# Row maxima of two heads in the two halves of TensorE's rows, later value products, and an unrolled expert loop

## The chip, the cores and the metric

The kernel runs on one core of a Trainium2 chip. The time is device microseconds of one execution of the whole program. TensorE (PE) multiplies, its weight loads are listed as PEld; VectorE is DVE, ScalarE is ACT, GpSimd is POOL, SyncE is SP and issues most DMAs. TensorE's clock has two levels, 1.2 and 2.4 GHz; a granted clock of 1.00 is the upper one.

## The reference, cut to what matters

A two-layer block over 4 sequences of 1024 tokens, width 256. Layer 0 is a linear attention and a mixture of 8 experts (2 for each token), layer 1 a causal softmax attention with 16 heads of 16 columns and a mixture of 16 experts (4 for each token) with a shared expert. The two parts that the change touches are

```python
# layer 1 attention: B=4, S=1024, 16 heads, d_head=16
scores = jnp.einsum('bqhd,bkhd->bhqk', Q, K)
scores = jnp.where(causal[None, None], scores, -jnp.inf)
attn = jax.nn.softmax(scores.astype(jnp.float32), axis=-1)
out = jnp.einsum('bhqk,bkhd->bqhd', attn, V).reshape(B, S, D)
# both layers, for each expert: 352 = 2*176 columns up, 176 down
h = silu(x @ w1[:, :176]) * (x @ w1[:, 176:])
y = h @ w2
```

The experts are computed on sorted tokens only: each tile of 128 tokens belongs to one expert, there are 71 such tiles in layer 0 and 143 in layer 1.

## The kernel before, in words

**Routed tiles** (`sparse_experts`, called for both layers). For each tile PE transposes x (2 instructions, L708), multiplies up (6 matmuls with 352 columns, L719), transposes h (2, L730) and multiplies down (6 with 256 columns, L742). Each fp32 product is three passes of high and low halves, which ACT and DVE split. The stages are staggered by `in_steps`: in step n PE does `transpose(n)`, `up(n-1)`, `transpose_h(n-2)`, `down(n-3)`. The matmuls read their weights at a register that holds the tile's expert. PE gets those registers from `te` with one TENSOR_LOAD (L694) at the head of each block of eight tiles: 8 registers at first, 11 in each turn of the hardware loop (`Fori`), 10 in the last part.

**Causal attention** (`causal_attention`). 16 rounds of 4 heads each (4 groups of heads, 4 sequences). In a round there are twelve steps of one 128-row key tile against one 512-column chunk of queries; of each step PE computes the four heads' scores (`scores`, L1508, up to 512 columns, three PSUM banks `psS`), ACT takes exp to `PT`, POOL cuts the diagonal (`cuts`), and PE multiplies by the values (`values`, L1520, four heads in four column groups of the array, 128 rows by 32 columns each). exp needs the maximum of each row, which is found a round ahead: *units* of at most one PSUM bank with queries as rows (`unit`, L1486 matmuls over 126 rows, of which 64 carry data, and a bf16 mask matmul L1493 for the diagonal), each reduced by DVE (L1399). There are 38 units for a round, 608 in all. The order within a step is written out by hand:

```python
ORDER = "0u1u2u3uv"     # digit: scores of that head, u: a unit of a later round, v: the values of the step before
```

Three slots hold the rounds' QS, KS and VA; `psM` has three banks, `psX` takes the transposes of the maxima (L1501) and of the outputs (L1535). After a round's last step the values of step 11, their copy to `OT` by DVE (L1424), the transposes and `divide` (L1429, L1433) follow before the next round begins. In step 6 DVE finishes the maxima of the next round (`whole`, L1408 and L1409) and PE transposes them. SP issues the loads (`pull`), the maxima's way through DRAM (`maxima_rows`) and the stores (`output`).

Of the kernel before, what the change touches and what calls it, by code (L numbers as in the profile page):

```python
# [12 lines left out]
F32 = mybir.dt.float32  # L13
# [169 lines left out]
def in_steps(eng, *stages, tiles=TILES, first=None, begin=None):  # L183
# [11 lines left out]
    if begin:  # L195
        begin(0, first)
    for n in range(first):
        step(n)
    with eng.Fori(first // POS_TILES, whole) as b:
        if begin:  # L200
            begin(b * POS_TILES, POS_TILES)
# [4 lines left out]
    if begin:  # L206
        begin(whole * POS_TILES, tiles + most - whole * POS_TILES)
# [438 lines left out]
def sparse_experts(nc, tag, E, NT, te, w_hi, w_lo, xs_dram, ys_dram, ident, shared=None):  # L646
# [3 lines left out]
    with phase(nc, shared) as (ctx, block):  # L650
# [37 lines left out]
        def _(pe):  # L688
            owners = {}

            def load_owners(n, count):
                before = 0 if isinstance(n, int) and n == 0 else 3
                count = min(count + before, NT - n + before) if isinstance(n, int) else count + before
                _, values = nc.values_load_multi_w_load_instructions(te[0:1, bass.ds(n - before, count)], (pe.engine,), min_val=0, max_val=E - 1,  # L694
                                                                      skip_runtime_bounds_check_because="a count of ends, cut to E - 1 where it is written")
                owners.clear()
                owners.update({j - before: v for j, v in enumerate(values)})

            def owner(i, lag):

                return owners[(i + lag) % POS_TILES - lag]
# [9 lines left out]
            def up(t, i, b):  # L711
                e = owner(i, 1)
# [20 lines left out]
            def down(t, i, b):  # L733
                e = owner(i, 3)
# [12 lines left out]
            in_steps(pe, (0, transpose), (1, up), (2, transpose_h), (3, down), tiles=NT, begin=load_owners)  # L747
# [486 lines left out]
def causal_attention(nc, qk_dram, v_dram, ident, mask_qk, ident_b, m_dram, ao_dram, pos, rows, xs_dram, sent, routing):  # L1234
# [7 lines left out]
    SLOTS = 3  # L1242
    with phase(nc) as (ctx, block):
# [8 lines left out]
        PT = sb("PT", [P, 2, GH, CHUNK])  # L1252

        units = [(qt, k0, w, h0, min(CHUNK // w, GH)) for qt in range(POS_TILES)
                 for k0, w in [(k, min(CHUNK, (qt + 1) * P - k)) for k in range(0, (qt + 1) * P, CHUNK)]
                 for h0 in range(0, GH, min(CHUNK // w, GH))]
# [11 lines left out]
        assert NS * GH % SLOTS == 0  # L1268
# [7 lines left out]
        waited = sb("waited", [1, 3])  # L1276
        o_sb = sb("o_sb", [P, 2, TPC, GH, D])

        psM = [ctx.enter_context(nc.psum_tensor(f"ca_psM{i}", [P, CHUNK], F32)) for i in range(SLOTS)]
        psS = [ctx.enter_context(nc.psum_tensor(f"ca_psS{i}", [P, CHUNK], F32)) for i in range(SLOTS)]  # L1280
# [616 lines left out]
```

## Time and profile before

| what | value |
|---|---|
| median of 3 runs | 2127.53 us (2126.42 to 2137.63) |
| profiled execution, own time | 2133.09 us |
| its span, first to last instruction | 2130.9 us |
| mean granted TensorE clock | 0.920 |
| PE busy | 1723.5 us, 81% |
| DVE busy | 1387.3 us, 65% |
| ACT busy | 946.3 us, 44% |
| POOL busy | 672.5 us, 32% |

The program is a row of stages with barriers between them: the experts of layer 0 run from about 460 to 640 us, the causal attention from 812 to 1446 (its first maxima start at 859, its first scores at 893), the experts of layer 1 from 1524 to 1894. A stage's time is set by what waits in it, so each is read by itself. A row of the timeline gives start, duration, engine, line, operation, operands with partitions and elements, the number of merged instructions and, in brackets, how long the engine had been idle and who ended that. Durations of matmuls are modelled and overlap; the distance from start to start is what PE takes.

### The profile page before, as it was taken

To read this page: it belongs to the slowest core of one execution; us is meant where nothing else is said; L and a number is where in the kernel's file an instruction comes from. 1 tells how busy PE (TensorE), PEld (TensorE's weight loads), DVE (VectorE), ACT (ScalarE), POOL (GpSimd) and SP (SyncE) were. 2 spreads that over 40 slices of the span, in tenths; PEclk is the share of its full clock that TensorE was granted. 3 is DMA by queue.
4 is the path that set the end of the run, shared out by engine and by line. 5 is a ranking of instruction groups with operands and counts; after the bars stand their busy time and mean duration, and the time that the engine had idled before them with its cause. 6 is when DMAs were issued, how large, how long until landed. Compare 5 with 4: busy or idle time off the path is not lost. (4 is left out here: it accounts for less than half of the span.)

```text
span 2130.9 us, 36160 instructions
## 1 busy us (share of the span) xinstructions
PE 1723.5 (81%) x10296; PEld 1331.0 (62%) x10297; DVE 1387.3 (65%) x2825; ACT 946.3 (44%) x2201; POOL 672.5 (32%) x850
## 2 busy tenths in 40 slices
PE   3999985638892780899999999995688988879997
PEld 2877874428881560455555555543588888868886
DVE  4589996315564876977777777723455656546766
ACT  0455652313343651166666656663333434333343
POOL 1455621730006824044343434340000000027760
PEclk9999997869995895899999999998899999989999
DMA  6445523623333996235353535317633333356661
GB/s 224 156 125 172 152 43 84 223 87 96 104 99 119 321 352 191 69 97 134 93 138 90 145 82 148 82 49 208 187 96 103 103 99 110 99 177 191 200 191 53
DMA packets 288496, 292.61 MB, mean 137 GB/s; under 512 B 122665, under 2 KB 245034, under 8 KB 286300
## 3 DMA queue, kind: packets, MB, share of 16 engines
q1 hardware_dynamic: 265340, 236.62, 37.9%
q0 software_dynamic: 18432, 50.36, 7.5%
q10 hardware_dynamic: 4608, 4.20, 0.6%
q8 instruction: 59, 0.97, 0.2%
q14 instruction: 57, 0.47, 0.1%
HBM read 144.97 MB, written 141.82 MB: 135 GB/s over the span
## 5 line engine op out<-in xcount | busy, mean ns | idle before, releaser
L1473 ACT ACTIVATE ca_PT<-ca_psS 128x512 f32<-128x512 f32 (+3 forms) x768 | 344.9, 493 | 273.1 <-PE ca_psS L1508 259.7
L1399 DVE TENSOR_REDUCE ca_part<-ca_psM 128x1 f32<-128x512 f32 (+3 forms) x608 | 368.5, 656 | 85.3 <-PE ca_psM L1493 60.7
L1508 PE MATMUL ca_psS<-ca_QS,ca_KS 128*128 128x512 f32 (+3 forms) x768 | 306.1, 409 | 4.1 <-ACT ca_PT L1473 4.1
L801 POOL DMA_INDIRECT g_y<-ys_scratch,pos x128 | 130.7, 1021 | 501.9 <-POOLq L68 456.5
L1486 PE MATMUL ca_psM<-ca_KS,ca_QS 126*128 126x512 f32 (+3 forms) x768 | 247.1, 365 | 15.9 <-issue 13.7
L1508 PEld LDWEIGHTS ca_psS<-ca_QS,ca_KS 128*128 128x128 f32 x768 | 147.7, 195 | 106.4 <-ACT ca_PT L1473 101.3
L776 DVE TENSOR_TENSOR f_x_lo<-f_psT,f_x_hi 128x256 fp32r<-128x256 f32 x214 | 90.9, 425 | 162.2 <-ACT f_x_hi L755 157.6
L755 ACT ACTIVATE f_x_hi<-f_psT 128x256 fp32r<-128x256 f32 x214 | 82.3, 385 | 248.0 <-PE f_psT L708 247.7
L708 PE MATMUL f_psT<-ident,f_xs 128*128 128x128 f32 x428 | 89.2, 293 | 113.8 <-issue 56.9
L719 PE MATMUL f_psU<-ffn_hi,f_x_hi 128*128 x428 | 164.8, 385 | 1.0 <-DVE f_x_lo L776 1.0
L1486 PEld LDWEIGHTS ca_psM<-ca_KS,ca_QS 126*128 126x128 f32 x768 | 141.4, 194 | 37.4 <-DVE ca_part L1399 14.3
L1520 PE MATMUL ca_psO<-ca_PT,ca_VA 128*32 128x512 f32 (+3 forms) x1536 | 160.7, 497 | 1.3 <-POOL ca_PT L1379 1.3
L781 DVE TENSOR_TENSOR f_h<-f_h,f_psU 128x176 f32<-128x176 f32 x214 | 72.3, 338 | 118.5 <-ACT f_h L761 118.5
L719 PE MATMUL f_psU<-ffn_hi,f_x_lo 128*128 x428 | 145.3, 340 | 0.0
L719 PE MATMUL f_psU<-ffn_lo,f_x_hi 128*128 x428 | 144.7, 338 | 0.0
L742 PE MATMUL f_psY<-ffn_hi,f_h_hi 88*128 x428 | 142.9, 334 | 0.0
L630 POOL DMA_INDIRECT xs_scratch<-x_sb,pos x128 | 123.3, 963 | 36.8 <-issue 36.8
L1377 POOL TENSOR_TENSOR ca_waited<-ca_waited 1x1 f32<-1x1 f32 x128 | 23.4, 183 | 342.0 <-ACT ca_PT L1473 342.0
L501 PE MATMUL fa_psO<-fa_weighed,ident 128*128 128x256 f32 x512 | 123.9, 398 | 9.1 <-DVE fa_weighed L360 9.0
L761 ACT ACTIVATE f_h<-f_psU 128x176 f32<-128x176 f32 x214 | 68.0, 318 | 141.5 <-PE f_psU L719 141.5
L708 PEld LDWEIGHTS f_psT<-ident,f_xs 128*128 128x128 f32 x428 | 54.3, 149 | 120.3 <-issue 62.0
L742 PE MATMUL f_psY<-ffn_hi,f_h_lo 88*128 x428 | 123.2, 288 | 0.0
(258 smaller groups left out, 4386.6 us busy)
## 6 DMA issues: line engine op xcount, KB each, us to landing
f_xs<-xs_scratch SPq DMA_DIRECT2D x214, 128.0 KB, 2.0
ys_scratch<-f_ys SPq DMA_DIRECT2D x214, 128.0 KB, 1.7
xs_scratch<-fa_blank SPq DMA_DIRECT2D x32, 640.0 KB, 4.0
ca_QS<-qk_scratch SPq DMA_DIRECT2D x32, 512.0 KB, 6.7
ca_KS<-qk_scratch SPq DMA_DIRECT2D x32, 512.0 KB, 8.1
po_raw<-in_ffn SPq DMA_DIRECT2D x24, 608.0 KB, 4.8
xs_scratch<-fa_blank SPq DMA_DIRECT2D x32, 384.0 KB, 3.4
v_scratch<-gp_v_st SPq DMA_DIRECT2D x32, 256.0 KB, 3.8
```

The source lines that it names most:

```text
L501: ins = pe.matmul(psO[i % 2][:, 0:NQ], ident[:], weighed[:, i % 2, g, :], start=g == 0, stop=g == KV_HEADS - 1)
L630: pool.indirect_dma_start(xs_dram, bass.IndirectOffsetOnAxis(pos[:, tile, k:k + 1], 0), rows[:, tile, :], None)\
L708: ins = pe.transpose(psT[i % 2][:, k * P:(k + 1) * P], xs[:, i % XR, k * P:(k + 1) * P], ident[:])
L719: ins = pe.matmul(psU[i % 2][:, 0:WU], x[:, i % 2, k * P:(k + 1) * P], w[:, bass.ds(e, 1), k * WU:(k + 1) * WU].rearrange("p a n -> p (a n)"),
L742: ins = pe.matmul(psY[i % 2][:, 0:HID], x[:, i % 2, k * P:(k + 1) * P], w[0:HALF, bass.ds(e, 1), first:first + HID].rearrange("p a n -> p ...
L776: dve.tensor_tensor(x_lo[:, i % 2, :], psT[i % 2][:, 0:HID], x_hi[:, i % 2, :].bitcast(F32), ALU.subtract)\
L801: pool.indirect_dma_start(dst[:, k, :], None, y_dram, bass.IndirectOffsetOnAxis(pos[:, tile, k:k + 1], 0)).then_inc(got, 16)
L1399: dve.tensor_reduce(dst, psM[(slot * NU + u) % SLOTS][:, 0:nh * w].rearrange("p (h k) -> p h k", h=nh), AX.X, ALU.max)\
L1473: act.activation(PT[:, s % 2, h, off:CHUNK], psS[(GH * s + h) % SLOTS][:, off:CHUNK], ACT.Exp)\
L1486: ins = pe.matmul(bank[:, h * w:(h + 1) * w], QS[0:STACK, slot, h0 + h, qt * P:(qt + 1) * P], KS[0:STACK, slot, h0 + h, k0:k0 + w], start= ...
L1508: pe.matmul(psS[tile % SLOTS][:, off:CHUNK], KS[:, slot, h, kt * P:(kt + 1) * P], QS[:, slot, h, c * CHUNK + off:(c + 1) * CHUNK], start=T ...
L1520: ins = pe.matmul(psO[STRIP * h:STRIP * (h + 1), off:CHUNK], VA[:, slot, kt, STRIP * h:STRIP * (h + 1)], PT[:, s % 2, h, off:CHUNK], start ...
```

## The change

In `sparse_experts` PE's loop is written out in Python: no hardware loop, and the expert's register is loaded by one TENSOR_LOAD of one register for each tile, placed after `up` and before `transpose_h`. The other engines keep their loops. In `causal_attention`:

- the units' operands get tiles of their own, QM and KM, with the 64 data rows of two heads in rows 0 to 63 and 64 to 127. A unit is now a pair: for each of its heads two matmuls over 64 rows, one in each half, into two PSUM banks, two masks where it touches the diagonal, and one reduction over both banks. 38 units become 20;
- `psM` is two pairs of banks, shared with the transposes of maxima and outputs, taken in a fixed order (`place`); `psX` is gone;
- the order of a step is "0u12u3v", and v is the values of two steps before; `PT` has three buffers;
- the values of a round's last two steps, and the second half's output, fall into the next round (step 2), the first half's output into step 6;
- two slots in place of three; 8 more loads for a round (`pull_pairs`).

```diff
-def in_steps(eng, *stages, tiles=TILES, first=None, begin=None):
+def in_steps(eng, *stages, tiles=TILES, first=None):
...
-            def load_owners(n, count):
...
+            def load_owner(t, i, b):
+                _, values = nc.values_load_multi_w_load_instructions(te[0:1, t:t + 1], (pe.engine,), min_val=0, max_val=E - 1,
...
+                owners.clear() if t == 0 else owners.pop(t - 4, None)
+                owners[t] = values[0]
...
-            in_steps(pe, (0, transpose), (1, up), (2, transpose_h), (3, down), tiles=NT, begin=load_owners)
+            for n in range(NT + 3):
+                for lag, stage in ((0, transpose), (1, up), (0, load_owner), (2, transpose_h), (3, down)):
+                    if lag <= n < NT + lag:
+                        stage(n - lag, (n - lag) % POS_TILES, (n - lag) // POS_TILES)
...
-    SLOTS = 3
+    SLOTS, PAIRS, PTS = 2, GH // 2, 3
...
+        QM, KM = sb("QM", [P, SLOTS, PAIRS, SEQ], F32R), sb("KM", [P, SLOTS, PAIRS, SEQ], F32R)
...
-        ORDER = "0u1u2u3uv"
+        ORDER = "0u12u3v"
...
+        OUT = [(s + 3) % NS for s in (max(s for s, (c, _, _) in enumerate(steps) if c == cc) for cc in range(SPAN))]
...
+            def pull_pairs(n):
+
+                slot = n % SLOTS
+                if n >= SLOTS:
+                    sp.wait_ge(pair_filled, place["unit", n - SLOTS, NU - 1] + 1)
+                rows = qk_dram[:, :, n, :, :].rearrange("c s (r g h) n -> s g r c (h n)", g=2, h=PAIRS)
+                for g in range(2):
+                    for half in range(2):
...
+                dst = part[:, k0 // CHUNK, :, qt].rearrange("p (g h) -> p g h", g=2)[:, :, p0:p0 + nh]
+                src = psM[at % 2][:, :, 0:nh * w].rearrange("p g (h k) -> p g h k", h=nh)
...
                 for h in range(nh):
-                    ins = pe.matmul(bank[:, h * w:(h + 1) * w], QS[0:STACK, slot, h0 + h, qt * P:(qt + 1) * P],
-                                    KS[0:STACK, slot, h0 + h, k0:k0 + w], start=True, stop=not diag, skip_group_check=True)
+                    for g in range(2):
+                        half = slice(g * P // 2, (g + 1) * P // 2)
+                        ins = pe.matmul(pair[:, g, h * w:(h + 1) * w], QM[half, n % SLOTS, p0 + h, qt * P:(qt + 1) * P],
+                                        KM[half, n % SLOTS, p0 + h, k0:k0 + w], start=True, stop=not diag, skip_group_check=True)
...
                         elif part == "v":
-                            if s:
-                                values(n, slot, s - 1)
+                            if n * NS + s >= PTS - 1:
+                                values(*divmod(n * NS + s - (PTS - 1), NS))
...
+                    if s == OUT[1] and n:
+                        transpose_out(n - 1, 1)
+                    if s == OUT[0]:
                         transpose_out(n, 0)
-                    if s == WHOLE - 1:
+                    if s == WHOLE - 1 and n + 1 < ROUNDS:
                         transpose_maxima(n + 1)
```

## Rows read from the trace of the kernel before

**Rows 1.** One attention round: us, PE, PEld, DVE, ACT, POOL busy, clock, DMA share, GB/s.
```profile
942.26:977.14 34.88, 33.78 (x227) 18.55 (x223) 26.74 (x49) 21.76 (x48) 13.81 (x25) 1.00 0.45 119
```

**Rows 2.** PE's waits in layer 1's experts: us in total, times, longest.
```profile
PE f_psT L708 <- issue: 39.2, 17, 2.5
```

**Rows 3.** Timeline of PE in both expert stages: first instruction of some tiles.
```profile
480.47 0.43 PE L708 MATMUL f_psT<-ident,f_xs 128*128 128x128 f32 x2 [2.14 <-issue]
...
625.11 0.41 PE L708 MATMUL f_psT<-ident,f_xs 128*128 128x128 f32 x2 [1.46 <-issue]
...
1545.83 0.43 PE L708 MATMUL f_psT<-ident,f_xs 128*128 128x128 f32 x2 [2.16 <-issue]
...
1588.08 0.68 PE L708 MATMUL f_psT<-ident,f_xs 128*128 128x128 f32 x2 [2.30 <-issue]
...
1611.21 0.38 PE L708 MATMUL f_psT<-ident,f_xs 128*128 128x128 f32 x2
...
1613.33 0.38 PE L708 MATMUL f_psT<-ident,f_xs 128*128 128x128 f32 x2
...
1873.64 0.41 PE L708 MATMUL f_psT<-ident,f_xs 128*128 128x128 f32 x2 [1.61 <-issue]
```

**Rows 4.** Line L694 in three windows: duration ns min/median/max, first and last start.
```profile
L694 PEldq TENSOR_LOAD <-te x1: 602/602/602, 1524.5 to 1524.5; - x1
...
L694 PEldq TENSOR_LOAD <-te x1: 2984/2984/2984, 1584.8 to 1584.8; - x1
...
L694 PEldq TENSOR_LOAD <-te x1: 2632/2632/2632, 1870.8 to 1870.8; - x1
```

**Rows 5.** Timeline of an expert tile: the last input of `up`, and its first matmul.
```profile
1582.21 0.42 DVE L776 TENSOR_TENSOR f_x_lo<-f_psT,f_x_hi 128x256 fp32r<-128x256 f32 x1 [0.20 <-ACT f_x_hi L755]
...
1583.65 0.40 PE L719 MATMUL f_psU<-ffn_hi,f_x_hi 128*128 x1
```

**Rows 6.** Timeline of PE in the first attention: a matmul over 2 rows between others over 128.
```profile
283.84 0.33 PE L99 MATMUL fa_psQ<-wqkvr_hi,fa_st_lo 128*128 128x384 f32 x1
284.10 0.44 PE L470 MATMUL fa_psQ<-fa_b_two,fa_ones 2*128 2x384 f32 x1
284.48 0.33 PE L99 MATMUL fa_psV<-wqkvr_hi,fa_st_hi 128*128 128x136 f32 x1
284.64 0.28 PE L99 MATMUL fa_psV<-wqkvr_lo,fa_st_hi 128*128 128x136 f32 x1
```

**Rows 7.** Timeline of PE in the causal attention: scores behind values, and units.
```profile
904.72 0.50 PE L1508 MATMUL ca_psS<-ca_QS,ca_KS 128*128 128x512 f32 x1
905.05 0.40 PE L1486 MATMUL ca_psM<-ca_KS,ca_QS 126*128 126x512 f32 x1
905.29 0.40 PE L1508 MATMUL ca_psS<-ca_QS,ca_KS 128*128 128x512 f32 x1
...
919.24 0.40 PE L1486 MATMUL ca_psM<-ca_KS,ca_QS 126*128 126x512 f32 x1
...
919.78 0.40 PE L1486 MATMUL ca_psM<-ca_KS,ca_QS 126*128 126x512 f32 x1
```

**Rows 8.** Timeline of the weight loads of one group of value products.
```profile
904.36 0.16 PEld L1520 LDWEIGHTS ca_psO<-ca_PT,ca_VA 128*32 128x32 f32 x8 [0.37 <-issue]
```

**Rows 9.** Timeline of PE at a round's end, in step 5 and in step 6.
```profile
962.57 0.66 PE L1535 MATMUL ca_psX<-ident,ca_OT 128*128 128x128 f32 x4 [0.81 <-DVE ca_OT L1424]
...
977.14 0.66 PE L1535 MATMUL ca_psX<-ident,ca_OT 128*128 128x128 f32 x4
...
981.43 0.28 PE L1501 MATMUL ca_psX<-ident,ca_maxima 128*32 128x128 f32 x1 [0.26 <-DVE ca_maxima L1409]
```

**Rows 10.** Timeline of DVE in steps 5 and 6.
```profile
978.13 0.42 DVE L1433 TENSOR_TENSOR ca_o_sb<-ca_psX,ca_rsum 128x256 f32<-128x256 f32 x1
...
980.98 0.37 DVE L1408 COPY ca_maxima<-ca_part 128x16 f32<-128x16 f32 x1
```

**Rows 11.** DMA issues of the attention: times, KB each, median us to landing.
```profile
ca_VA<-v_scratch SPq DMA_DIRECT2D x16, 512.0 KB, 10.8
```

More of the change, by code:

```diff
@@ L1304, in first, with next_place @@
-        def first(n):
-            return isinstance(n, int) and n == 0
+        LOADS, PAIR_LOADS = 5, 8
+        place = {}
+        def next_place(*x):
+            place[x] = len(place)
+        for u in range(NU):
+            next_place("unit", 0, u)
+        next_place("maxima", 0)
+        for u in range(FIRST):
+            next_place("unit", 1, u)
+        for n in range(ROUNDS):
+            for s in range(NS):
+                for u in ahead[s]:
+                    if n + 1 + s // WHOLE < ROUNDS:
+                        next_place("unit", n + 1 + s // WHOLE, u)
+                if s == OUT[1] and n:
+                    next_place("out", n - 1, 1)
+                if s == OUT[0]:
+                    next_place("out", n, 0)
+                if s == WHOLE - 1 and n + 1 < ROUNDS:
+                    next_place("maxima", n + 1)
@@ L1307, in _, with pull @@
+        next_place("out", ROUNDS - 1, 1)
+        masked, slots_done = routing((ctx, block), PT[:, :, :, :].rearrange("p a h n -> p (a h n)"), psO)
         @block.sync
         def _(sp):
-            def pull(n, slot):
-                at = sp.snap(n) if not isinstance(n, int) else n
-                if not (isinstance(n, int) and n < SLOTS):
-                    sp.wait_ge(oT_done, (n - SLOTS + 1) * SPAN)
-                rows = qk_dram[:, :, bass.ds(at, 1), :, :].rearrange("c s a (r h) n -> s r c (a h n)", h=GH)
+            def pull(n):
+                slot = n % SLOTS
+                if n >= SLOTS:
+                    sp.wait_ge(pair_filled, place["out", n - SLOTS, 1] + 1)
+                rows = qk_dram[:, :, n, :, :].rearrange("c s (r h) n -> s r c (h n)", h=GH)
@@ L1426, in divide @@
             def divide(n, c):
[L1427 to L1428 removed]
+                at = place["out", n, c]
+                dve.wait_ge(pair_filled, at + 1)
+                o4 = psM[at % 2][:, 0, :].rearrange("p (q h d) -> p q h d", q=TPC, h=GH)
                 dve.reciprocal(rsum[:, :, :], o4[:, :, :, D]).then_inc(sum_done, 1)
                 dve.wait_ge(sum_done, n * SPAN + c + 1)
[L1431 removed]
+                if n:
@@ L1444, in both @@
                         collect(n, 0)
-                    if s == last_step[0] + 2:
+                    if s == OUT[0]:
                         divide(n, 0)
-                    if s == WHOLE - 1:
+                    if s == WHOLE - 1 and n + 1 < ROUNDS:
                         whole(n + 1)
-                collect(n, 1)
-                divide(n, 1)
-            def front():
-                for u in range(NU):
-                    unit(0, 0, u)
-                whole(0)
-                for u in range(FIRST):
-                    unit(1, 1, u)
@@ L1459, in back @@
-            def back(n, slot, turn):
-                for c in range(SPAN):
-                    collect(n, c)
-                    divide(n, c)
-            rounds(dve, both, front, back)
+            collect(ROUNDS - 1, 1)
+            divide(ROUNDS - 1, 1)
         @block.scalar
@@ L1516, in values @@
                     pe.wait_ge(exp_done, n * (GH * NS) + GH * s + GH)
-                if kt == 0 and not (first(n) and c == 0):
+                if kt == 0 and (n or c):
                     pe.wait_ge(ot_out, n * SPAN + c)
@@ L1525, in transpose_out @@
             def transpose_out(n, c):
+                pair = banks(place["out", n, c])
                 pe.wait_ge(ot_out, n * SPAN + c + 1)
-                if c == 0:
-                    if not first(n):
-                        pe.wait_ge(o_out, n * SPAN)
-                else:
-                    pe.wait_ge(o_out, n * SPAN + 1)
-                    if not (isinstance(n, int) and n == ROUNDS - 1):
-                        pe.wait_ge(m_neg, n + 2)
-                for q in range(TPC):
-                    ins = pe.transpose(psX[:, q * P:(q + 1) * P], OT[:, q * P:(q + 1) * P], ident[:, :])
```

257 lines of the change are left out of this document (120 added, 137 removed).

## The prediction

> **What bounds the kernel now.** The two touched stages are read one by one, first by busy time in stretches, then by PE's waits, then in the timeline.
>
> In the attention a round takes 34.88 us, and PE is busy for 33.78 of them against 26.74 for DVE and 21.76 for ACT, at the full clock [rows 1]. So PE's issue order is the bound: whatever adds or takes time from start to start on PE moves the stage.
>
> In the experts PE is the bound too, but with a hole at the head of each block of eight tiles: 17 waits of together 39.2 us in layer 1, put down to "issue" [rows 2], and holes of the same kind in layer 0. No engine is late there. The line of the register load tells why: a TENSOR_LOAD of 11 registers starts at 1584.8, takes 2.98 and ends at 1587.8, and PE's next matmul is at 1588.08 after 2.30 idle [rows 3, 4]. An undisturbed tile takes 1613.33 - 1611.21 = 2.12 [rows 3]. Layer 1's blocks from 1545.83 to 1873.64 are 16 x 8 = 128 tiles in 327.8 us, and 128 x 2.12 = 271.4: 56.4 lost. Layer 0's 56 tiles from 480.47 to 625.11 take 144.6 against 118.7: 25.9 lost. The two holes before these stretches add 2.14 + 2.16 [rows 3]. Together **86.6 us** are lost to the heads of blocks: the larger part as idle time (2.3 for each of 25 heads [rows 2]), the rest as restarts and as the lower clock that follows most holes (the first transposes take 0.68 at 1588.08 against 0.38 at 1611.21).
>
> **The expert loops: -86 us if the load is hidden.** The change replaces 27 loads of 8 to 11 registers with 214 of one. What does one cost? The loads of before bound it [rows 4]: 8 registers took 0.60 while PE was idle, 10 took 2.63 and 11 took 2.98 while it was working; 0.08 to 0.27 for a register, and at most 0.60 if the shortest load is all fixed cost. I take 0.3. It occupies PE's sequencer, not the array, so it is free while matmuls are queued. The sequencer is ahead there: `up` waits for x_lo, which is done at 1582.21 + 0.42 = 1582.63, and `up`'s first matmul runs at 1583.65 [rows 5], so its six matmuls are queued about 1.0 before the first one runs, and they last another 0.95. With about 0.5 for handing over six matmuls and their address registers (an estimate: the rest of the lead less this), the load has some 1.3 us of cover. Behind it in the queue stand `transpose_h` and `down`, whose inputs are then ready. Cost taken: 0. If that cover were gone, each 0.1 us exposed would cost 214 x 0.1 = 21 us. The other engines keep their loops; they have slack (a tile's x_lo is 1.0 early), so what they lose at a turn of the loop stays hidden. The clock should then stay up through the stage. **Term: -86**, bounds -87 and, with 0.15 exposed for each tile, -54.
>
> The Trainium skill, DMA: Bandwidth & Descriptors (section on latency and other measured facts), gives a register load a floor of about 600 ns. By that a load of one register would take 0.6; this is still under the cover, and the sum would not change. The trace agrees as far as it goes: 602 ns for the shortest [rows 4].
>
> **The maxima on PE: +2.8 us a round.** Matmuls over half of the rows run two at once, but they stand between scores over all 128 rows. What such a change of shape costs is shown by a matmul over 2 rows among others over 128 [rows 6]: from 283.84 to 284.64, 0.80 us, for 384 + 384 + 136 columns, which at 2.4 GHz are 0.16 + 0.16 + 0.06 = 0.38. One excursion costs **0.42**: twice the array has to empty, and twice a weight load isn't covered by the matmul before. The values, in four column groups, show half of it: the score of 512 columns behind them takes 905.05 - 904.72 = 0.33 to the next matmul [rows 7], where a unit of 512 columns among its like takes 905.29 - 905.05 = 0.24.
>
> Before, a unit of 512 columns costs those 0.24, two heads 0.47. After, the pair streams at once: 0.21 + 0.42 = 0.63, so +0.16. That takes the two weight loads as concurrent, as the eight of a group of values are over in 0.16 altogether [rows 8]. Units on the diagonal: 919.78 - 919.24 = 0.54 for unit, mask and a score of 384 columns [rows 7], less 0.17 for the score, is 0.37, two heads 0.74; after, 0.21 + 0.42 + two masks of 256 columns 0.21 = 0.84, +0.10. Those with 384 columns: 0.64 becomes 0.79; those with two narrow heads in each half cost 0.12 to 0.15 more than before. A round has 8 pairs without mask and 12 with one: 8 x 0.16 + 12 x 0.12 = **+2.8**. From below: if a change of shape costs nothing, a pair is 0.24 and the 20 units take 7.7 in place of 12.4, -4.7. From above: if the halves' matmuls don't overlap at all, 0.21 more for a pair and somewhat more with two heads, +5 on top, +7.8. I take the middle, because the 2-row matmul is the same kind of change [rows 6].
>
> **The round's end and step 6: +0.6 us a round.** Taken away is PE's wait of 0.81 for the copy to OT [rows 9]. But the values of steps 10 and 11, which ran as one group, become two, one more excursion, at some 0.3 (0.42 less most of one weight load, since the values' are of 32 columns [rows 8]): -0.5. In step 6 the output's transposes and `divide` now stand ahead of the maxima. By the starts there and on DVE [rows 9, 10], divide's second instruction starts 0.99 after the transposes and takes 0.42 (978.13, 977.14), then L1408 and L1409 need 981.43 - 980.98 = 0.45 to PE's start, less 0.07 by which L1408 can start early: the maxima's transpose comes 1.8 after the output's, and PE has 0.42 of work in between. It idles 1.35 where it idled 0.26: +1.1. Behind it on PE is everything of step 7.
>
> **The rest.** DVE's 20 reductions of 1024 elements do the work of 38 of 512, and DVE stays under 27 of some 38 us. `psM` is two deep, but pairs come every 1.8 us on average and a reduction takes 1.2. Values two steps behind take waits off ACT and POOL, which PE hardly has. SP issues 8 more DMAs in a round, 2.1 MB beside the 4.2 that 119 GB/s move in 34.88 us; DMA share 0.45 becomes about 0.7 [rows 1]. They are issued a round ahead, `pull` from step 2 for the next round, some 28 us against the 10.8 of the slowest load [rows 11]; SP waits there with the stores and maxima behind it, all of which have steps to spare. The first maxima wait for DVE's routing, as before. These: -2 in all, for the front and for the last boundary.
>
> Units lie in about 14.6 rounds' worth: 14.6 x (2.8 + 0.6) - 2 = **+48**.
>
> **Sum**: -86 + 48 = **-38**. The profiled execution took 2133.1 (span 2130.9), so it gives 2095; the median of the runs shown is 2127.5, which gives **2089**.
>
> **Rivals.**
> - *Changing shape is cheap, the maxima gain.* For it: two matmuls over different rows can't disturb each other. Against: the measured excursions [rows 6, 7]. Then (-4.7 + 0.6) x 14.6 - 2 = -62, in all -148: 1980; half-way, 2035. The Trainium skill, TensorEngine Tiling (Array Packing), Overview, promises up to 2x for a contraction of 64 or less. By that the units' 7.7 us of streaming per round would halve, some -3.8 a round; the same page warns that a change of mode drains the array, and the 0.42 of [rows 6] bears out the warning.
> - *The halves don't overlap, or their weight loads come one after the other.* Another 0.11 for a pair (loads alone) to 0.26: +2.5 to +5 a round, +36 to +73, so 2125 to 2162. Against: the weight loads of column groups [rows 8].
> - *Slower: the register load waits until the array is empty.* Then PE idles in each tile for the load and the restart. For it: loads took 2.6 to 3.0 while PE was working and 0.60 when idle, and 1.40 of the 2.63 lie after PE's last matmul (1870.8 + 2.63 = 1873.43, less 1873.64 - 1.61). Against: that does not scale from 0.60 to 1.40 and 2.0 by registers either. Price: 0.3 to 0.6 and a restart of 0.25, times 214: +118 to +182, with the rest 2205 to 2270. It decides from 0.18 us exposed for a tile (38 / 214), where the gain is gone.
>
> **How the numbers follow.** The forecast (2065 to 2110 by the spread of its terms) has 0.52, cheap changes of shape 0.13, no overlap 0.15, the exposed load 0.20. The range takes in no overlap, half of the cheap case and partly exposed loads: 2010 to 2195. What this kernel's measurement can tell from no change is about 0.5%, 10.6 us: 2117 to 2138 is "same". Faster: 0.50 + 0.13 + 0.04 of no overlap = 0.67; same 0.09; slower 0.24.
>
> **What would show it.** Expert tiles 2.12 apart throughout with a TENSOR_LOAD in each and no "issue" waits; if the load waits, a hole of 0.5 to 0.9 in every tile behind `up`. In the attention, the distance from a score over a 512-column pair to the next score: 0.85 (0.21 for the score itself and 0.63), with the two matmuls starting together; a round of 38.3 us; no wait for OT at a round's end, 1.3 us of idle before L1501's successor. A round under 34.9, or tiles with holes, would make the prediction wrong.

## The result, and the profile after

The changed kernel takes **2078.7 us** (median of 4 runs, 2066.8 to 2087.0), the kernel before beside it 2127.0 (4 runs). The ratio is **0.976**, 95% interval 0.9724 to 0.9796. The forecast was 2089, 38 us less than before; it came to 48 less. The profiled execution is the slowest of the four, 2087.0, with a span of 2085.2. Ratios, here and below, leave out executions over 1.5% above the fastest of their kernel, which drops four of the six in run 10 and none elsewhere.

The stages by windows, first the kernel before, from a stage's first to its last matmul (us, then PE, PEld, DVE, ACT and POOL busy, granted clock, DMA share, GB/s):

```profile
0.00:460.80 460.80, 322.57 (x1508) 268.63 (x1509) 303.38 (x497) 183.43 (x387) 204.65 (x206) 0.90 0.46 142
460.80:644.40 183.60, 165.28 (x1136) 158.86 (x1136) 105.20 (x283) 72.08 (x214) 0.00 (x0) 0.92 0.33 99
...
844.60:1444.80 600.20, 560.37 (x3572) 303.98 (x3572) 441.11 (x812) 344.93 (x768) 221.15 (x384) 0.98 0.40 103
1444.80:1526.50 81.70, 43.78 (x194) 33.05 (x193) 34.93 (x50) 30.32 (x48) 0.00 (x0) 0.81 0.83 235
1526.50:1894.40 367.90, 328.18 (x2288) 316.60 (x2288) 212.25 (x572) 143.46 (x430) 0.00 (x0) 0.94 0.33 101
```

The same of the changed kernel:

```profile
0.00:464.40 464.40, 326.01 (x1508) 271.35 (x1508) 301.79 (x497) 183.33 (x387) 204.12 (x206) 0.89 0.45 141
464.40:619.40 155.00, 154.38 (x1136) 150.13 (x1136) 104.96 (x283) 71.40 (x214) 0.00 (x0) 0.98 0.40 118
...
819.50:1459.10 639.60, 596.42 (x3604) 271.35 (x3604) 419.10 (x525) 344.79 (x768) 221.21 (x384) 0.94 0.57 145
1459.10:1542.70 83.60, 43.89 (x192) 33.35 (x192) 34.97 (x50) 30.41 (x48) 0.00 (x0) 0.84 0.80 230
1542.70:1848.60 305.90, 305.37 (x2288) 298.33 (x2288) 211.66 (x571) 141.89 (x430) 0.00 (x0) 0.99 0.41 122
```

The expert stages: 155.0 - 183.6 = -28.6 and 305.9 - 367.9 = -62.0, together **-90.6**. The attention: 639.6 - 600.2 = **+39.4**. All the rest, which nothing touches, +5.5 (3.6 of it ahead of the first expert stage). Sum -45.7, which is 2085.2 - 2130.9.

**Experts.** PE's waits in layer 1's stage (what answers to [rows 2]):

```profile
PE f_psT L696 <- DMA f_xs<-xs_scratch: 7.2, 2, 6.8
```

That is the stage's start; the 39.2 us of "issue" are gone. PE is busy for all of 1560 to 1840 at a clock of 1.00. All the loads together (to [rows 4]; ns min/median/max):

```profile
L686 PEldq TENSOR_LOAD <-te x214: 296/304/527, 464.4 to 1842.0; - x107
```

**A round of the attention** (to [rows 1]):

```profile
975.00:1011.69 36.69, 35.63 (x229) 16.48 (x225) 25.24 (x32) 21.70 (x48) 13.82 (x24) 1.00 0.67 167
```

36.69 in place of 34.88, at the same clock. PE is busy for 1.85 more and idle for 1.06 in place of 1.10, so the 1.81 are work on PE, not a wait. PE around a pair without a mask (to [rows 7]):

```profile
994.91 0.62 PE L1525 MATMUL ca_psS<-ca_QS,ca_KS 128*128 128x384 f32 x2
995.46 0.50 PE L1505 MATMUL ca_psM<-ca_KM,ca_QM 64*128 64x512 f32 x2
995.89 0.44 PE L1525 MATMUL ca_psS<-ca_QS,ca_KS 128*128 128x384 f32 x1
```

The two scores are of 384 columns, 0.16 each at 2.4 GHz. To the pair's start they take 0.55, to the next score 0.98: 0.98 - 0.32 = 0.66 for a pair, where the forecast had 0.63 and two units of before took 0.47. So an excursion to half rows and back costs 0.66 - 0.21 = 0.45, close to the 0.42 of [rows 6]. The two matmuls of the pair start 4 ns apart in the trace (995.462 and 995.466), and so do their weight loads, which are over in 0.18 together (to [rows 8]):

```profile
995.46 0.18 PEld L1505 LDWEIGHTS ca_psM<-ca_KM,ca_QM 64*128 64x128 f32 x2 [0.25 <-issue]
```

So the halves do run at once, and the rival in which they come one after the other is out.

A pair with masks costs less than was priced. Four scores of 512 columns with two such pairs take 2.65 in all:

```profile
1008.05 0.49 PE L1525 MATMUL ca_psS<-ca_QS,ca_KS 128*128 128x512 f32 x1
1008.48 0.50 PE L1505 MATMUL ca_psM<-ca_KM,ca_QM 64*128 64x512 f32 x2
...
1009.70 0.51 PE L1505 MATMUL ca_psM<-ca_KM,ca_QM 64*128 64x512 f32 x2
```

The step ends at 1010.70, with the first value product. In the kernel before the same work, four scores and four units with a mask each, runs from 942.68 to 945.23, which is 2.55. That is +0.05 for a pair, and the forecast had +0.10. From pair to pair, 1008.48 to 1009.70, it is 1.22, less 0.43 for the two scores: 0.79, priced 0.84.

Step 6 on PE, then on DVE (to [rows 9] and [rows 10]):

```profile
975.00 0.66 PE L1546 MATMUL ca_psM<-ident,ca_OT 128*128 128x128 f32 x4
976.72 0.27 PE L1518 MATMUL ca_psM<-ident,ca_maxima 128*32 128x128 f32 x1 [1.06 <-DVE ca_maxima L1427]
```

```profile
975.99 0.42 DVE L1452 TENSOR_TENSOR ca_o_sb<-ca_psM,ca_rsum 128x256 f32<-128x256 f32 x1
976.33 0.17 DVE L1426 COPY ca_maxima<-ca_part 128x16 f32<-128x16 f32 x1
```

The maxima's transpose comes 1.72 after the output's, behind `divide`. No wait for OT is left at the round's end.

**The front of the attention** is what the prediction had not priced. Windows of the kernel before, from the last routing instruction on DVE over the first maxima (883.7) and the first score (893.3) to the second maxima:

```profile
861.00:883.70 22.70, 19.86 (x66) 10.08 (x64) 22.33 (x41) 0.00 (x0) 0.00 (x0) 0.93 0.00 0
883.70:893.30 9.60, 9.21 (x38) 5.60 (x38) 8.96 (x18) 0.00 (x0) 0.00 (x0) 0.82 0.57 143
893.30:911.70 18.40, 18.29 (x118) 10.02 (x116) 15.76 (x29) 12.73 (x28) 9.72 (x15) 1.00 0.47 123
```

The same events in the changed kernel (first maxima 860.8, first score 874.4, second maxima 903.2):

```profile
836.00:860.80 24.80, 19.05 (x60) 6.93 (x61) 21.98 (x23) 0.00 (x0) 0.00 (x0) 0.50 0.02 5
860.80:874.40 13.60, 9.74 (x34) 3.65 (x34) 9.26 (x11) 0.00 (x0) 0.00 (x0) 0.50 0.80 180
874.40:894.60 20.20, 20.20 (x68) 9.41 (x72) 8.42 (x8) 8.18 (x20) 6.89 (x12) 0.50 0.52 131
894.60:903.20 8.60, 7.54 (x49) 3.09 (x41) 6.50 (x10) 4.87 (x9) 3.95 (x5) 0.98 0.21 76
```

Read the clock's column: before it rises within the first window, after it stays at 0.50 (1.2 GHz) through the front and another 20.2 us in which PE is never idle. From the stage's first matmul to the second maxima it is 911.7 - 844.6 = 67.1 before, 903.2 - 819.5 = 83.7 after: **+16.6**. Of these 2.2 lie ahead of the first maxima, 4.0 between them and the first score, and 10.4 behind it, where the half clock is.

The 4.0 are not the clock's. The maxima go through DRAM on their way to the scores, and the time from issue to landing of their first store was, before and after,

```profile
m_scratch<-ca_m_hi SPq DMA_DIRECT2D x1, 16.0 KB, 2.0
```

```profile
m_scratch<-ca_m_hi SPq DMA_DIRECT2D x1, 16.0 KB, 7.3
```

In the changed kernel SP issues eight of the pairs' loads, of 256 KB each, just ahead of this store, and the first score waits for the maxima at the end of the way:

```profile
PE ca_psS L1525 <- DMA ca_QS<-m_scratch: 3.2, 1, 3.2
```

In every trace with the pairs' loads the store takes 6.4 to 7.5 and the first score comes 13.6 to 14.2 behind the maxima; in every trace without them it is 1.4 to 2.0 and 9.0 to 11.3. No run moved these loads alone.

Then 14 rounds of 1.82 more are +25.5, and the end from the last maxima (42.0 in place of 44.7) -2.7: together +39.4.

### The profile page after: what moved, and what is told of

Read it like the earlier page. It is cut to its first block and busy times, and to the rows that moved or that the text cites. A ratio compares the mean times of both kernels' runs of the same rounds, so it can differ in the third digit from the quotient of the medians.

```text
span 2085.2 us, 35991 instructions
## 1 busy us (share of the span) xinstructions
PE 1726.9 (83%) x10328; PEld 1273.2 (61%) x10328; DVE 1365.1 (65%) x2537; ACT 944.2 (45%) x2201; POOL 665.2 (32%) x848
## 5 line engine op out<-in xcount | busy, mean ns | idle before, releaser
L1420 DVE TENSOR_REDUCE ca_part<-ca_psM 128x2 f32<-128x1024 f32 (+2 forms) x320 | 349.4, 1116 | 160.6 <-PE ca_psM L1511 116.9
L1525 PE MATMUL ca_psS<-ca_QS,ca_KS 128*128 128x512 f32 (+3 forms) x768 | 273.4, 413 | 7.2 <-ACT ca_PT L1486 3.9
L1525 PEld LDWEIGHTS ca_psS<-ca_QS,ca_KS 128*128 128x128 f32 x768 | 132.3, 192 | 147.0 <-ACT ca_PT L1486 100.3
L1505 PE MATMUL ca_psM<-ca_KM,ca_QM 64*128 64x512 f32 (+3 forms) x768 | 165.0, 454 | 17.4 <-DVE ca_part L1420 17.2
L707 PE MATMUL f_psU<-ffn_hi,f_x_hi 128*128 x428 | 156.9, 367 | 0.5 <-DVE f_x_lo L767 0.5
L707 PE MATMUL f_psU<-ffn_hi,f_x_lo 128*128 x428 | 139.3, 326 | 0.0
L707 PE MATMUL f_psU<-ffn_lo,f_x_hi 128*128 x428 | 138.3, 323 | 0.0
L696 PE MATMUL f_psT<-ident,f_xs 128*128 128x128 f32 x428 | 83.8, 278 | 60.2 <-DMA f_xs<-xs_scratch 60.2
L1505 PEld LDWEIGHTS ca_psM<-ca_KM,ca_QM 64*128 64x128 f32 x768 | 71.1, 196 | 94.6 <-issue 47.9
L730 PE MATMUL f_psY<-ffn_lo,f_h_hi 88*128 x428 | 120.8, 282 | 0.0
```

The source lines that it names most:

```text
L707: ins = pe.matmul(psU[i % 2][:, 0:WU], x[:, i % 2, k * P:(k + 1) * P], w[:, bass.ds(e, 1), k * WU:(k + 1) * WU].rearrange("p a n -> p (a n)"),
L730: ins = pe.matmul(psY[i % 2][:, 0:HID], x[:, i % 2, k * P:(k + 1) * P], w[0:HALF, bass.ds(e, 1), first:first + HID].rearrange("p a n -> p ...
L1420: dve.tensor_reduce(dst, src, AX.X, ALU.max).then_inc(pair_taken, 1)
L1505: ins = pe.matmul(pair[:, g, h * w:(h + 1) * w], QM[half, n % SLOTS, p0 + h, qt * P:(qt + 1) * P], KM[half, n % SLOTS, p0 + h, k0:k0 + w], ...
L1525: pe.matmul(psS[tile % BANKS][:, off:CHUNK], KS[:, slot, h, kt * P:(kt + 1) * P], QS[:, slot, h, c * CHUNK + off:(c + 1) * CHUNK], start=T ...
```

## Experiments

Each edit is against the changed kernel unless it says otherwise. "Ratio" is against the kernel before on the same chip. Runs 5 to 8, the second run of 6, the first of 9 and run 10 were on three chips on which the kernel before took 2303 to 2328. The stages that read most from memory took long there (300 us for 213 in the last stage of run 5), and even the attention of before needed 40.3 us for a round (run 5), so rounds and totals there say little of PE. The expert stages can still be read (155 and 307 in run 6, as in run 1), and so can the front's clock.

**1. The written-out expert loop alone**, on the kernel before.

```
-            in_steps(pe, (0, transpose), (1, up), (2, transpose_h), (3, down), tiles=NT, begin=load_owners)
+            for n in range(NT + 3):
+                for lag, stage in ((0, transpose), (1, up), (0, load_owner), (2, transpose_h), (3, down)):
```

> The kernel before with the written-out expert loop on PE alone. Theory: the two halves of the change lie in different stages and add up. By the two profiles the expert stages fell from 183.6 and 367.9 us to 155.0 and 305.9, together 90.6 less, so this kernel should take 2127 - 91 = 2036, its expert stages 155 and 306, tiles 16.93 us for eight, the granted clock 1.00 in them, and its attention rounds 34.88. Rival: part of the expert gain needs the other half of the change, or a warmer stage of experts costs clock elsewhere; then it takes 2050 or more, or a stage that neither half touches is longer than before.

Measured: 2040.3 (2033.1 to 2042.3) against 2130.4, ratio 0.9574, 0.9547 to 0.96. Expert stages 155.0 and 306.8, attention 599.0. The two halves add up, and this half alone is better than the whole change (0.976).

**2. The changed attention alone**, with the expert loop of before.

> The changed attention with the expert loop of before. Theory: the attention phase takes 639.6 us as in the changed kernel, against 600.2, so this kernel takes 2127 + 39 = 2166, rounds of 36.70, and the first 20 us of round 0 at half the clock. Rival: the half clock at the attention's front comes from the experts before it, which ran at full clock without a hole; then the front has its full clock here, the phase is some 12 us shorter, and the kernel takes 2154.

Measured: 2173.1, ratio 1.0193, 1.016 to 1.0226. The attention's rounds are 36.70. The stage takes 635.9, experts 183.9 and 367.9. From the stage's start to the second maxima it is 80.0, at 0.50 until some 10 us behind the first score. So the half clock doesn't come from the experts without holes, but how long it lasts behind the first score differs from run to run: about 10 us here and in run 3, 18 to 20 in the changed kernel's profiled execution and in runs 4 and 7. From the first score to the second maxima it takes 24.5 and 23.9 in the former, 28.4 to 29.6 in the latter. That is 4 to 5 us; the changed kernel's four times are 20 apart, and what makes up the rest isn't known.

**3. The load ahead of `up`.**

```
-                for lag, stage in ((0, transpose), (1, up), (0, load_owner), (2, transpose_h), (3, down)):
+                for lag, stage in ((0, transpose), (1, load_owner), (1, up), (2, transpose_h), (3, down)):
```

The load is now that of the very tile that `up` multiplies next.

> The changed kernel with the one-register load ahead of up instead of behind it. Ahead of it only the four-pass transposes of one tile are queued, and up's six matmuls with their address registers wait for it. Theory (cover): the load of 0.30 and the handing over are no longer hidden behind up's own queued matmuls; if all 0.30 is exposed each tile takes 2.42 in place of 2.12, and the kernel 214 x 0.30 = 64 us more, 2143; if the queue runs far enough ahead here as well, tiles stay at 2.12 and the time at 2079. Rival (the load needs an empty array): tiles of 2.12 in the changed kernel already speak against it; it would give holes of 0.9 in each tile here, 2270.

Measured: 2073.0 (2066.5 to 2081.9), ratio 0.9738, 0.9703 to 0.9773; eight tiles in 16.93 as in the changed kernel. A load of 0.30 is hidden in this place too, so it needs less cover than `up`'s six matmuls gave it.

**4. Eight registers for each tile**, of which one is used.

```
-                _, values = nc.values_load_multi_w_load_instructions(te[0:1, t:t + 1], (pe.engine,), ...
+                _, values = nc.values_load_multi_w_load_instructions(te[0:1, t:min(t + 8, NT)], (pe.engine,), ...
```

> The changed kernel with eight registers loaded for each tile, in the same place behind up, though only the first is used. It tells what made the loads of before long, 0.60 for 8 registers with PE idle and 2.6 to 3.0 for 10 and 11 with PE at work. Theory A (number of registers): 8 take 0.6 here too, under 1.3 us of cover, tiles stay at 2.12 and the time at 2079. Theory B (work on the array slows the load): 8 registers take 2 us or more, at least 0.7 of it is exposed for each tile, and the kernel takes 2079 + 214 x 0.7 = 2229 or more.

Measured: 2314.3, ratio 1.0859, 1.0829 to 1.0889; the expert stages take 229.5 and 468.2. Two loads of this run, the first from entry 14 and the second from entry 16, a multiple of four (duration in ns):

```profile
L686 PEldq TENSOR_LOAD <-te x1: 2142/2142/2142, 1642.5 to 1642.5; - x1
...
L686 PEldq TENSOR_LOAD <-te x1: 598/598/598, 1649.9 to 1649.9; - x1
```

Both have PE at work beside them. The 598 ns load leaves its tile at 2.12 and the 2142 ns one makes a tile of 3.7. Behind the latter PE idles for 1.33 until 0.17 after the load's end, so 0.8 of its 2.14 cost nothing. Neither theory survives as it was put: it is not the number alone (both load 8) and not work on the array (both have it). The pattern is strict: loads from entries 0, 4, 8, ... take 0.60, the three between 1.9 to 2.2. The last loads of layer 0, of 7, 5 and 3 registers, show the steps:

```profile
L686 PEldq TENSOR_LOAD <-te x1: 1075/1075/1075, 659.1 to 659.1; - x1
...
L686 PEldq TENSOR_LOAD <-te x1: 1275/1275/1275, 664.8 to 664.8; - x1
...
L686 PEldq TENSOR_LOAD <-te x1: 787/787/787, 670.2 to 670.2; - x1
```

Five are 5 x 0.255 and three are 3 x 0.262; seven begin at entry 64 and cost 1.075, less than the 1.275 of five from entry 66: a group of four at 0.30 and three at 0.26. So a register costs 0.26 to 0.27, but when the load itself starts at an entry that divides by four, each four registers come together in 0.30. A load that starts elsewhere has no such groups, though it passes over entries that divide by four. The loads of before fit: 11 x 0.27 = 2.97, 10 x 0.265 = 2.65, and 8 from entry 0 in 2 x 0.30 [rows 4].

**5. The kernel before, its loads started one entry earlier.**

```
-                before = 0 if isinstance(n, int) and n == 0 else 3
+                before = 0 if isinstance(n, int) and n == 0 else 4
```

> The kernel before, loop and attention as they were, with one number changed: each block's load begins four tiles back in place of three, so 12 registers from an entry whose index divides by four. In the run with eight registers for each tile, every fourth load (index 0, 4, 8, ...) took 0.60 and the others 1.9 to 2.2; the last loads of layer 0, of 7, 6, 5, 4, 3, 2 and 1 registers, took 1.08, 1.60, 1.27, 1.00, 0.79, 0.53 and 0.30. Theory (start): a register costs 0.27, but four that begin at such an index come in 0.30 together; then this load takes 0.9 in place of 3.0, the holes shrink from 2.3 to 0.3 or less, the clock stays up, and the kernel takes 2127 less 60 to 85, 2042 to 2067. Rival (number): 12 registers take 3.2 or more, the holes grow by 0.3, and the kernel takes 2127 + 25 x 0.3 = 2135.

Measured: ratio 0.9733, 0.9679 to 0.9788 (2266.3 against 2328.2 on that chip). One of its loads, then a block's head, then the waits of layer 1's stage:

```profile
L694 PEldq TENSOR_LOAD <-te x1: 1053/1053/1053, 1653.6 to 1653.6; - x1
```

```profile
1654.90 0.43 PE L708 MATMUL f_psT<-ident,f_xs 128*128 128x128 f32 x2 [0.37 <-issue]
```

```profile
PE f_psT L708 <- issue: 6.4, 16, 0.5
```

One register more, and the load takes 1.05 in place of 3.0; the hole is 0.37 in place of 2.3 and the clock is 1.00 from 1640 to 1800. The expert stages take 158.7 and 318.1, together 74.7 less than before, against 90.6 for the loop written out. Four fifths of the expert gain were one digit away, without a loop written out. The whole kernel gained 62 of the 60 to 85 expected, on a chip that is slower throughout.

**6. Whole rows for the maxima**, the order of work and the reductions as changed.

```
-                        half = slice(g * P // 2, (g + 1) * P // 2)
-                        ins = pe.matmul(pair[:, g, h * w:(h + 1) * w], QM[half, n % SLOTS, p0 + h, qt * P:(qt + 1) * P],
+                        ins = pe.matmul(pair[:, g, h * w:(h + 1) * w], QS[0:STACK, n % SLOTS, g * PAIRS + p0 + h, qt * P:(qt + 1) * P],
```

with `SLOTS = 3` and without the pairs' loads.

> The changed kernel with its order of work, its two-bank tiles and its reductions of 1024 elements, but each head's product for the maxima over all 126 rows, one after the other, from the stacks that the scores use (three of them again, no pairs' loads). It takes only the half-row packing back. Theory (the packing costs in changes of shape): scores, units and masks take 23.5 + two masks' worth of 0.5 in place of 25.05 in a round, so rounds of 35.2 to 35.6 in place of 36.70, 16 to 22 us less; 2057 to 2063 where the changed kernel takes 2079. Rival (the packing is free and the order or the reductions cost): rounds stay at 36.7. Of the front: if its half clock comes from the pairs on half of the rows, it is gone here and 12 more us are saved; if it comes from waiting for the reductions, it stays.

Measured: ratio 0.9667, 0.9604 to 0.973; rounds of 41, where 35.2 to 35.6 was expected, whose length tells nothing (see above). PE's busy time in one of them is 36.05, against 38.03 with half rows on the same chip (run 7), at clocks of 0.95 and 0.92. Of the front: its clock is 0.64 over 860 to 880, 0.50 from 880 to 885 and 1.00 from 890 on, into round 0, where the pairs stay at 0.50; from the stage's start to the second maxima it takes 75.5, against 84.7 for the pairs (run 7) and 69.2 for the attention of before (run 5) on the same chip. Both theories of the front hold in part here: whole rows give PE more to do between the reductions. But this run also leaves out the pairs' loads, and its first score comes 10.0 behind the maxima in place of 13.8. The same kernel again:

> The kernel of e_full_rows once more, since on the chip where that ran even the attention of before took 40 us for a round, so its rounds told nothing of PE. Theory (the half-row pairs' changes of shape cost more than the pairs save): rounds of 35.2 to 35.6 in place of 36.70, the starts of scores, units and masks on PE 24.0 us apart in sum in place of 25.05; and the front is again at its full clock from the first scores on, so the attention phase takes 605 to 612 in place of 635 to 640 and the kernel 2050. Rival (the pairs are free, the order of work costs): rounds of 36.7.

Measured: ratio 0.9745, 0.9712 to 0.9778, again with rounds of 41 and not conclusive.

**7. The output's transposes one step later.**

```
-                    if s == OUT[0]:
+                    if s == OUT[0] + 1:
                         transpose_out(n, 0)
```

(and `divide` and the bank's turn with it)

> The changed kernel with the first half's output transposes and their division one step later, behind step 7 in place of step 6, so that they don't stand ahead of the maxima. Theory: of the 1.06 idle in step 6 some 0.8 go, a round takes 35.9, and the kernel 16 x 0.8 = 13 less, 2066. Rival: the bank that the transposes take then holds up step 8's pairs, or the maxima wait for the two-deep banks instead; the round stays within 0.2 of 36.7.

Measured: ratio 0.9687, 0.9616 to 0.9758, rounds of 40.9, expected 35.9, with a wait of 2.8 for the maxima in which DVE starts its reductions late. Not conclusive by itself; run 9 answers.

**8. The front's products computed twice**, into the same place.

```
-                for h in range(nh):
+                for h in list(range(nh)) * times:
```

> The changed kernel with each product for the maxima of round 0 and of the first part of round 1, before the first scores, computed twice into the same place, so that PE has no idle time between the reductions there. Theory (PE's idling keeps the clock at 0.50 through the front and 10 to 20 us into round 0): the clock rises within the front, round 0 runs at 1.00, and the attention phase takes 625 to 630 in place of 635 to 640, though PE has more to do. Rival: the clock is held down by something else (its half rows, the loads that run beside it); then the front only gets longer, by up to 27 x 0.4 = 11 us, and the kernel takes 2090.

Measured: ratio 0.9695, 0.9634 to 0.9757. Windows over the same events as above (last routing instruction, first maxima 875.4):

```profile
855.00:860.00 5.00, 4.27 (x20) 1.57 (x20) 4.14 (x4) 0.00 (x0) 0.00 (x0) 0.77 0.00 0
860.00:875.40 15.40, 10.47 (x69) 4.79 (x69) 14.56 (x16) 0.00 (x0) 0.00 (x0) 1.00 0.04 9
```

The clock rises between 855 and 860 and stays at 1.00 until the first maxima and the products of round 1 behind them are done. Then PE waits 5.4 for the maxima's way through DRAM, and the clock falls again: 0.80 from 885 to 890, 0.52 from 890 to 895, 1.00 after that. From the stage's start to the second maxima it takes 79.7 against 84.7 on the same chip with the products done once (run 7), though PE does more. So PE's idling between the reductions held the clock down, not the half rows. But the 5.0 all lie behind the first score (24.4 for 29.6): the first maxima come 41.2 after the stage's start and the first score 14.1 after them, as with the half clock (41.3 and 13.8). The attention of before takes 69.2 on this chip, so two thirds of the front's loss are left.

Two pairs next to each other at this clock, and what follows them:

```profile
871.46 0.73 PE L1505 MATMUL ca_psM<-ca_KM,ca_QM 64*128 64x512 f32 x4 [0.40 <-DVE ca_part L1420]
872.13 0.39 PE L1511 MATMUL ca_psM<-mask_qk,ident_b 128*128 128x256 bf16 x2
```

That is 0.67 for two, 0.33 for a pair, against 0.66 for the pair between scores and 0.47 for its two products over whole rows.

**9. Whole rows, later transposes and the doubled front together.**

> Three edits on the changed kernel together, each with its own place in the trace: whole rows for the maxima, the output's transposes one step later, and the front's products computed twice. Theory: rounds of 35.4 less 0.8 of idle in step 6, 34.6, so 0.3 under before's 34.88; a front at 1.00 from about its fifth product on; the attention phase 593 to 600, and the kernel 2035 to 2042, no worse than the written-out experts with the attention of before (2040). Rival: the idle in step 6 turns into a wait for the two-deep banks and the round stays at 35.4; then 2050.

Measured on one of the chips told of above: ratio 0.9733, 0.9697 to 0.9769. Once more:

> The kernel of e_rows_later_front once more, as it too ran on a chip where the attention of before takes over 40 us for a round. Theory: rounds of 34.2 to 34.6 (before 34.88, changed 36.70), the granted clock at 1.00 from the middle of the front on, the attention phase 593 to 600 in place of 600 (before) and 635 to 640 (changed), and the kernel 2035 to 2042. Rival: without the half-row pairs the round is still above 35.5, so the order of the work or the two-bank tiles carried the cost, not the pairs; then 2055.

Measured, on a chip on which the kernel before takes 2134.1: 2129.9, ratio 0.9993, 0.9968 to 1.0019. The expected 2035 was missed by 95. Windows of this run, in the front, over the one round that nothing delayed, and over one of the others:

```profile
835.00:845.00 10.00, 9.48 (x45) 6.01 (x44) 8.45 (x9) 0.00 (x0) 0.00 (x0) 0.97 0.00 0
888.16:922.90 34.74, 33.84 (x226) 19.48 (x226) 25.03 (x31) 21.51 (x48) 13.83 (x24) 1.00 0.33 84
1004.45:1044.90 40.45, 36.08 (x225) 20.54 (x226) 25.24 (x31) 21.48 (x48) 13.82 (x24) 0.92 0.35 97
```

PE in the latter, and PE's waits over the rounds from 888 on:

```profile
1004.45 0.27 PE L1498 MATMUL ca_psM<-ident,ca_maxima 128*32 128x128 f32 x1 [0.63 <-DVE ca_maxima L1408]
1008.20 0.80 PE L1505 MATMUL ca_psS<-ca_QS,ca_KS 128*128 128x512 f32 x1 [3.48 <-DMA ca_VA<-v_scratch]
```

```profile
PE ca_psS L1505 <- DMA ca_VA<-v_scratch: 56.5, 13, 5.6
```

The delay was my own edit's: with whole rows the maxima need the third stack by step 7, but its load now waited for the output two steps into the round. 3.3 to 5.6 us of waiting, and part of a round at half the clock behind it. The one undisturbed round carries the answer: PE busy for 33.84 with whole rows, 35.63 with half rows, in the same order and with the same two-bank tiles. **The half-row pairs cost 1.79 us of PE a round**, 0.09 for each of 20, and whole rows in the new order are level with the 33.78 of before. A pair of products without a mask over whole rows, in the same place as the half-row pair shown above:

```profile
906.17 0.51 PE L1505 MATMUL ca_psS<-ca_QS,ca_KS 128*128 128x384 f32 x2
906.52 0.62 PE L1485 MATMUL ca_psM<-ca_KS,ca_QS 126*128 126x512 f32 x2
906.97 0.34 PE L1505 MATMUL ca_psS<-ca_QS,ca_KS 128*128 128x384 f32 x1
```

From score to score 0.80 in place of 0.98, so 0.48 for the two products in place of 0.66. Over the three steps that hold only plain pairs, six of them, half rows take 0.88 more, 0.15 for each. The idle in step 6 went from 1.06 to 0.63, half of what was expected of the later transposes.

**10. The same with the stack's loads ahead of the store.**

```
-                    sp.wait_ge(pair_filled, place["out", n - SLOTS, 1] + 1)
+                    sp.wait_ge(s_done, (n - SLOTS + 1) * (GH * NS))
```

(the queries and keys, issued before the store of the round's second half; the values keep the old wait, behind it)

> e_rows_later_front with the loads of the next stack of queries and keys issued as soon as the last scores of the round before are done, ahead of the store of that round's second half, and the values' load behind that store. In the run before, these loads were issued at 1034.67 and PE waited 3.5 to 5.6 us for the last of them in eleven of eleven rounds, with half the clock behind each wait, while the one round without such a wait took 34.74. Theory (that wait was all that was wrong): every round takes 34.6 to 34.8, 2 us less than the changed kernel's 36.70, the attention phase 590 to 600, and the kernel 2030 to 2042. Rival: the rounds of 40 to 41 had another cause, and this one stays above 36; then it takes 2065 or more.

Measured: six executions from 2183.4 to 2228.9, median 2217.9, against 2303.2, on another of those chips. The two fastest, 2183.4 and 2206.2, give the ratio of 0.9527, 0.9455 to 0.96; with all six it would be 0.963. The profile is of an execution of 2218.5. The wait for the stack is gone from every round of it, so that was the loads; the rounds take 37.3 to 40.1, with a wait of up to 3.4 for the maxima, as the attention of before had in run 5 on another of these chips (up to 3.4). The 2030 to 2042 expected can't be tested on this chip, and the kernel can't be ranked against the written-out experts alone (0.9574, on a chip where the kernel before takes 2130). Whether a round takes 34.7 throughout stays open.

## Why the prediction was right

The sign and the size hold, the size in part by luck: two errors in the attention, of 24 and 16 us, went opposite ways.

- *The holes are the register loads, and one register is free*: right. Term -86, measured -90.6, above the bound of -87. The rows counted ended at the last head of each stage; what follows these heads (tiles of 3.4 and 2.5 in place of 2.12) also went. One register cost 0.30 as taken.
- *Its cover*: right in effect. It was put at 1.3; run 4 shows about 0.8 of a load of 2.14 covered and one of 0.60 hidden whole, and run 3 shows that 0.30 is hidden without it. By the Trainium skill, DMA: Bandwidth & Descriptors (section on latency and other measured facts), a register load has a floor of about 600 ns; the 214 loads of 0.30 disagree, and the measurement decides.
- *What the load's price depends on*: the prediction saw that the time doesn't follow the number of registers, and left it there. It follows the number and whether the load starts at an entry that divides by four (runs 4 and 5). With this, the cheaper edit was in sight.
- *The slower rival (the load waits for an empty array)*: refuted by loads of 0.30 and 0.60 with PE at work. A load of 2.1 does make its tile 1.5 longer (3.6 to 3.7 for 2.12), but through its length.
- *The maxima on PE, +2.8 a round*: the mechanism and the direction were right, the size too large. The price of an excursion, 0.42 from a 2-row matmul [rows 6], held: around a pair it is 0.66 - 0.21 = 0.45, and the plain pairs cost 0.15 more each (run 9), priced 0.16. The term that was mis-sized is the pairs with a mask. By the starts on PE, scores, units and masks take 1.58 of the round's 1.81; less 8 x 0.15 that leaves about 0.03 for each of the 12, where 0.12 was priced. The step shown above gives 0.05.
- *The round's end and step 6, +0.6*: wait gone as said, maxima 1.72 behind the output's transposes (1.8 foretold), idle 1.06 (1.35 foretold). The two cancel: PE's idle time in a round is as long as before. What is left of the round, 1.81 - 1.58 = 0.23, is near the 0.3 foretold for the values of steps 10 and 11 as two groups.
- *"The rest, -2, for the front and for the last boundary"*: wrong by 16. The front was +16.6 and the end -2.7. The prediction weighed DVE's larger reductions within a round alone; it missed that in the front PE, with less to do between them, would wait for them again and again (seven waits of 0.3 to 0.6 from 840 to 857), and that its clock would then stay at 0.50 into round 0. Run 8 shows the cause of the low clock: with PE kept at work it rises, which is worth 5.0. The prediction also gave the maxima behind the pairs' loads steps to spare, which they have within a round and not ahead of the first score: 4.0. The Trainium skill, TensorE: Matmul & The Clock Gate (section A second HAM failure mode: psum-queue depth-cycling), describes a kernel in which PE waits a little between groups of matmuls, cycling through PSUM banks, so often that the clock swings between its two levels. The waits here are of that kind, but the clock doesn't swing: it stays at 0.50 from 819.5 to 894.6.
- Net for the attention: forecast +48, measured +39.4. For the rounds it had 14.6 x 3.4 = 49.6 and they were 25.5, 24 less; front and end were 16 more.
- DVE stayed at 25.24 of a round and the DMA share rose to 0.67, as foretold; neither bounds anything.

## What to carry to other kernels

Before an engine's loop is written out because of a hole at its head, look at the length of the load there against its start and count: a start on a multiple of four took the same hole from 2.3 to 0.37 us. A packing of half rows must win more than the changes of shape around it: a pair took 0.33 next to its like and 0.66 between whole-row matmuls, where whole rows took 0.47. And a stretch that another engine paces can lose PE's clock when PE's own part in it gets cheaper, so the clock's column is read there as well, not only the waits. New loads are also checked against what stands behind them in the queue where nothing else hides it, at a stage's start.

## What the runs showed of the hardware

- A TENSOR_LOAD on PE's queue costs 0.26 to 0.27 us for a register, and 0.30 to 0.35 for each four when the load starts at an index divisible by four (8 in 0.60, 12 in 1.05, 11 from another start in 3.0). The 8 took 0.60 with PE idle (kernel before) and with PE at work (run 4).
- Two matmuls over 64 rows each, in the two halves, start 4 ns apart. Between matmuls over 128 rows the pair of 512 columns costs 0.66, 0.45 of it for the change of shape and back; next to another pair it costs 0.33 (run 8).
- With PE never idle, the clock stayed at 0.50 for 20.2 us behind the front in the changed kernel, 18 to 20 in runs 4 and 7, and about 10 in runs 2 and 3. What decides between the two isn't settled here.
- On three of the chips DVE sat idle for 1.4 to 1.6 us ahead of reductions whose inputs were ready, while GpSimd issued scatters (1.41 and 1.42 in run 5, 1.60 in run 10), and the rounds took 37 to 43 us. Why these chips differ from the others wasn't found.
